# Vision layer on one core: the attention memory term made per group inside the loop instead of ahead of it

## The reference, cut to what matters

```python
sq = jax.nn.elu(q) + 1.0
A_mem = jnp.einsum('bhsd,hde->bhse', sq, mem) / (jnp.einsum('bhsd,hdo->bhso', sq, z) + 1e-06)
g = jax.nn.sigmoid(betas)
out = g * A_mem + (1.0 - g) * attn
out = out.transpose(0, 2, 1, 3).reshape(b, s, d)
out = out @ Wo.T + bo
```

## Time and profile before

| what | value |
|---|---|
| median of 3 runs | 249.62 us (249.26 to 251.57) |
| the profiled execution | 249.06 us, its span 247.3 us |
| mean granted clock of PE over the span | 0.912 of full |
| PE busy | 210.5 us, 85% |
| DVE, ACT, POOL busy | 88.7, 76.2, 54.9 us |

### The profile page before, as it was taken

How to read it: one execution, slowest core, us unless ns; L and a number is a source line. 1 busy time by engine, 2 the same in 40 slices (tenths; PEclk the granted TensorE clock), 3 DMA queues, 4 the chain that set the end, 5 groups by cost and what they waited for, 6 DMA issues and landing times.

```text
span 247.3 us, 3565 instructions
## 1 busy us (share of the span) xinstructions
PE 210.5 (85%) x1307; PEld 187.7 (76%) x1307; DVE 88.7 (36%) x279; ACT 76.2 (31%) x224; POOL 54.9 (22%) x55
## 2 busy tenths in 40 slices
PE   0185956989998785989999999999999999999970
PEld 0185956965766454459999999999999999999970
DVE  6849874443678654203211111111111111111120
ACT  2433311634554114023622232322222323222220
POOL 0245343000004446300004004022040040220404
PEclk9999995995579855599999999999999999999997
DMA  7935995520001322167429058095290580410211
GB/s 247 337 117 127 322 351 233 215 98 1 0 21 41 97 61 65 51 170 238 199 62 447 2 212 314 0 358 184 70 439 10 223 305 0 170 12 0 23 9 17
DMA packets 10299, 36.15 MB, mean 146 GB/s; under 512 B 3328, under 2 KB 6738, under 8 KB 7978
## 3 DMA queue, kind: packets, MB, share of 16 engines
q1 hardware_dynamic: 7514, 31.90, 35.7%
q0 software_dynamic: 2336, 2.13, 4.4%
q10 hardware_dynamic: 432, 1.90, 2.0%
HBM read 31.42 MB, written 5.35 MB: 149 GB/s over the span
## 4 chain that ended last, share of the span: by engine, by line
PE 74%; DVE 8%; DMA 5%; issue 4%; POOL 4%; ACT 2%; POOLq 1%; SPq 0%
PE bank L538 33%; PE bank L550 16%; DMA x_flat<-in 5%; PE bank L582 3%; PE bank L522 3%; DVE hn L793 3%; PE bank L469 2%; POOL token_rows L1027 2%; PE bank L424 2%; POOL rstd L1014 1%; PE bank L437 1%; PE bank L563 1%; PE bank L388 1%; PE bank L449 1%; PE bank L390 1%
## 5 line engine op out<-in xcount | busy, mean ns | idle before, releaser
L538 PE MATMUL bank<-xb,w 128*128 128x185 f32 x512 | 91.5, 322 | 1.1 <-ACT xb L710 1.1
L538 PEld LDWEIGHTS bank<-xb,w 128*128 128x128 f32 x512 | 81.9, 190 | 1.6 <-issue 1.2
L977 DVE TENSOR_TENSOR hid<-bank,sg 128x185 f32<-128x185 f32 x64 | 22.5, 351 | 113.4 <-ACT sg L722 113.4
L550 PE MATMUL bank<-hid,w 128*128 128x185 f32 x256 | 50.2, 319 | 0.0
L1044 POOL DMA_INDIRECT out<-yw,slot_token x16 | 23.8, 1489 | 118.3 <-ACT yw L742 109.1
L722 ACT ACTIVATE sg<-bank 128x185 f32<-128x185 f32 x64 | 20.9, 326 | 89.2 <-PE bank L538 89.2
L550 PEld LDWEIGHTS bank<-hid,w 128*128 128x128 f32 x256 | 42.1, 189 | 0.0
L337 PE MATMUL bank<-wp_hi,x_hi 128*111 128x256 f32 x36 | 11.2, 310 | 12.3 <-DVE x_lo L799 12.3
L337 PEld LDWEIGHTS bank<-wp_hi,x_hi 128*111 128x111 f32 x36 | 7.0, 194 | 12.5 <-issue 12.5
L1027 POOL DMA_INDIRECT token_rows<-rowbuf,dest x12 | 11.6, 968 | 13.4 <-DVE dest L936 11.6
L1035 POOL TENSOR_TENSOR rstd<-var,minus_half 111x1 f32<-111x1 f32 (+1 forms) x6 | 3.4, 571 | 34.3 <-DVE var L908 34.2
(11 more groups left out here) (145 smaller groups left out, 265.9 us busy)
## 6 DMA issues: line engine op xcount, KB each, us to landing
w<-in SPq DMA_DIRECT2D x8, 2048.0 KB, 10.6
w<-in SPq DMA_DIRECT2D x8, 1024.0 KB, 4.8
x_flat<-in SPq DMA_DIRECT2D x6, 333.0 KB, 10.7
token_rows<-rows_in SPq DMA_DIRECT2D x1, 1728.0 KB
rows_in<-token_rows SPq DMA_DIRECT2D x8, 144.0 KB
w_sb<-in ACTq DMA_DIRECT2D x1, 1024.0 KB, 8.6
wp_sb<-in ACTq DMA_DIRECT2D x1, 768.0 KB, 5.5
out<-h SPq DMA_DIRECT2D x5, 111.0 KB
```

Of the source, the lines that this page charges most:

```text
L538: mm = pe.matmul(o, w[:, part, k, :], xb[b][:, k, :], start=(k == 0), stop=(k == KD - 1))
L550: mm = pe.matmul(bank[YT_BANK[k]][:, 0:NS], w3[e % 2][:, fc, k * P:(k + 1) * P], hid[:, step % 4, :], start=(fc == 0), stop=(fc == FC - 1))
L977: dve.tensor_tensor(hid[:, step % 4, :], bank[GU_BANK[step % len(GU_BANK)]][:, NS:2 * NS], sg[:, step % 2, :], ALU.mult).then_inc(hid_done, 1)
```

## The change

The memory term leaves the place ahead of the loop; only the denominators stay there, now after the first two scores. The gate no longer weighs the denominators: DVE multiplies it into `mem_bd` before q comes. In the loop PE has a new stage `remember(g)` (lag 3, between `project` and `count`), which makes sq @ mem for one group with tokens on the partitions, in the upper half of the attention product's bank. DVE has a new stage `weigh_memory(g)` (lag 3, between `row_max` and `rank`), which multiplies it by the reciprocal denominators. `attend` begins with three more matmuls: one of zeros that opens the bank, and two with the identity that turn the weighed memory term into it; the attention product then accumulates on top. The sum needs no addition any more, so DVE's `add_memory` goes and ACT copies the bank to `aoT` (`copy_ao`, lag 4, first in its tuple). The constant `head_rows`, its DMA and its cast, the turn of the denominators and their copies go too. The diff, cut where it only declares or renumbers:

```diff
--- before.py
+++ after.py
         qneg = sb1("qneg", [P, 2, T])
         sqT = sb1("sqT", [P, 2, T])
-        memT = qneg
         den = sb1("den", [G_ROWS, GROUPS, HEADS])
-        den_split = sb1("den_split", [G_ROWS, GROUPS, 2, HEADS], F32R)
-        denT = sb1("denT", [2 * HEADS, T], F32R)
-        memgate = in_x_space(P, 1, 2, HALF)[:, 0]
+        mem_rows = in_x_space(G_ROWS, 2, HEADS, HD)
         probs = in_x_space(G_ROWS, 2, HEADS, G_ROWS)
         probsT = in_x_space(G_ROWS, 2, HEADS, G_ROWS)
         negmax = sb1("negmax", [G_ROWS, GROUPS, HEADS])
...
@@ -263,6 +257,7 @@
         S_BANK = ((0, 1), (2, 3))
         PT_BANK = 4
         PV_BANK, WO_BANK = 5, 6
+        MEM_AT = 512 - D
         ROUTER_BANK = 7
 
         block = ctx.enter_context(nc.Block())
...
@@ -402,27 +396,17 @@
                                        start=(m == 0), stop=(m == 1))
                 mm.then_inc(den_in_psum, 1)
 
-            def memory_turn():
-
-                pe.wait_ge(den_done, 1)
-                for g in range(GROUPS):
-                    R = ROWS[g]
-                    b, c = g // (GROUPS // 2), g % (GROUPS // 2) * G_ROWS
-                    tr = pe.transpose(bank[4 + b][0:2 * HEADS, c:c + R],
-                                      den_split[0:R, g, :, :].bitcast(F32).rearrange("p s h -> p (s h)"), ident[0:R, 0:R])
-                tr.then_inc(denT_in_psum, 1)
-
-            def memory():
-
-                pe.wait_ge(denT_done, 2)
-                for n, (m, hf) in enumerate(WIDE):
-                    if n == 0:
-                        pe.wait_ge(k_done, 4)
-                    if n >= 2:
-                        pe.wait_ge(mem_done, n - 1)
-                    pe.matmul(bank[4 + n % 2][:, 0:HALF], head_rows_r[:, m, :], denT[:, half(hf)], start=True, stop=True)
-                    pe.matmul(bank[6 + n % 2][:, 0:HALF], mem_bd[:, m, :], sqT[:, m, half(hf)],
-                              start=True, stop=True).then_inc(mem_in_psum, 1)
+            def remember(g):
+
+                R = ROWS[g]
+                if g == 0:
+                    pe.wait_ge(mem_gated, 1)
+                else:
+                    pe.wait_ge(ao_done, g)
+                for m in range(2):
+                    mm = pe.matmul(bank[PV_BANK][0:R, MEM_AT + m * P:MEM_AT + (m + 1) * P], sqT[:, m, cols(g)], mem_bd[:, m, :],
+                                   start=True, stop=True)
+                mm.then_inc(mem_in_psum, 1)
 
             def score(g):
                 R = ROWS[g]
...
@@ -442,7 +426,7 @@
                 R = ROWS[g]
                 pe.wait_ge(pn_done, g + 1)
                 if g == 0:
-                    pe.wait_ge(mem_done, 4)
+                    pe.wait_ge(den_done, 2)
                 if g >= 1:
                     pe.wait_ge(pT_done, g)
                 for hd in range(HEADS):
@@ -451,13 +435,16 @@
 
             def attend(g):
                 R = ROWS[g]
+                pe.wait_ge(mem_done, g + 1)
+                pe.matmul(bank[PV_BANK][:, 0:2 * R], zero_bf[:, 0:P], zero_bf[:, 0:2 * R], start=True, stop=False, skip_group_check=True)
+                for m in range(2):
+                    pe.matmul(bank[PV_BANK][:, m * R:(m + 1) * R], mem_rows[0:R, g % 2, 2 * m:2 * m + 2, :].rearrange("p h c -> p (h c)"),
+                              ident[0:R, 0:R], start=False, stop=False, skip_group_check=True)
                 pe.wait_ge(pT_done, g + 1)
-                if g >= 1:
-                    pe.wait_ge(ao_done, g)
                 for hd in range(HEADS):
                     rows = slice(HD * (hd % 2), HD * (hd % 2) + HD)
                     mm = pe.matmul(bank[PV_BANK][rows, (hd // 2) * R:(hd // 2 + 1) * R],
-                                   v_sb[0:R, g, hd * HD:(hd + 1) * HD], probsT[0:R, g % 2, hd, 0:R], start=True, stop=True)
+                                   v_sb[0:R, g, hd * HD:(hd + 1) * HD], probsT[0:R, g % 2, hd, 0:R], start=False, stop=True, skip_group_check=True)
                 mm.then_inc(pv_done, 1)
 
             def project(g):
...
@@ -497,15 +484,13 @@
                 pe.wait_ge(hot_done, g + 1)
                 pe.matmul(o, before_bf[0:R, 0:R], hot[0:R, g, :], start=False, stop=True).then_inc(count_done, 1)
 
-            memory_den()
             pe.wait_ge(k_done, 4)
             pe.wait_ge(mask_set, 1)
             score(0)
             score(1)
-            memory_turn()
-            memory()
+            memory_den()
             for t in range(GROUPS + 7):
-                for lag, stage in ((6, route), (3, turn_probs), (4, project), (6, count), (5, turn_xn), (0, score), (3, attend)):
+                for lag, stage in ((6, route), (3, turn_probs), (4, project), (3, remember), (6, count), (5, turn_xn), (0, score), (3, attend)):
                     if 0 <= t - lag < GROUPS and not (stage == score and t - lag < 2):
                         stage(t - lag)
 
...
@@ -687,19 +672,17 @@
                                        scale=gamma_t[:, k:k + 1], bias=beta_t[:, k:k + 1])
                 a.then_inc(xnT_done, 1)
 
-            act.wait_ge(denT_in_psum, 1)
-            first = GROUPS // 2 * G_ROWS
-            act.activation(denT[:, 0:first], bank[4][0:2 * HEADS, 0:first], ACT.Copy).then_inc(denT_done, 1)
-            act.activation(denT[:, first:T], bank[5][0:2 * HEADS, 0:T - first], ACT.Copy).then_inc(denT_done, 1)
+            def copy_ao(g):
+                R = ROWS[g]
+                act.wait_ge(pv_done, g + 1)
+                if g >= 2:
+                    act.wait_ge(wo_done, g - 1)
+                act.activation(aoT[:, g % 2, :, 0:R], bank[PV_BANK][:, 0:2 * R].rearrange("p (m c) -> p m c", m=2),
+                               ACT.Copy).then_inc(ao_done, 1)
+
             softmax(0)
-            for n in range(len(WIDE)):
-
-                act.wait_ge(mem_in_psum, n + 1)
-                if n >= 2:
-                    act.wait_ge(mem_done, n - 1)
-                act.activation(memgate[:, n % 2, :], bank[4 + n % 2][:, 0:HALF], ACT.Copy).then_inc(memgate_done, 1)
             for t in range(GROUPS + 7):
-                for lag, stage in ((1, softmax), (5, copy_xnT), (2, copy_probsT)):
+                for lag, stage in ((4, copy_ao), (1, softmax), (5, copy_xnT), (2, copy_probsT)):
                     if 0 <= t - lag < GROUPS and not (stage == softmax and t - lag < 1):
                         stage(t - lag)
             GU_BANK, YT_BANK, XB_BANK, Y_BANK = (0, 1, 2, 7), (3, 4), 5, 6
...
@@ -840,7 +823,9 @@
             dve.wait_ge(gate_exp, 1)
             then(dve.tensor_scalar(gate[:, :], gate[:, :], 1.0, None, ALU.add))
             then(dve.reciprocal(gate[:, :], gate[:, :]))
-            then(dve.tensor_scalar(keep[:, :], gate[:, :], -1.0, 1.0, ALU.mult, ALU.add))
+            dve.tensor_scalar(keep[:, :], gate[0:G_ROWS, :], -1.0, 1.0, ALU.mult, ALU.add)
+            mem_heads = mem_bd[:, :, :].rearrange("p m (h c) -> p (m h) c", h=2)
+            dve.tensor_tensor(mem_heads, mem_heads, gate[:, :].unsqueeze(2).broadcast_to([P, HEADS, HD]), ALU.mult).then_inc(mem_gated, 1)
 
 
             for n, (m, hf) in enumerate(WIDE):
@@ -865,17 +850,19 @@
                 dve.wait_ge(den_in_psum, 1)
                 full = (GROUPS - 1) * HEADS
                 den2 = den[:, :, :].rearrange("p g h -> p (g h)")
-                dve.tensor_scalar(den2[:, 0:full], bank[4][0:G_ROWS, 0:full], 1e-6, None, ALU.add)
-                then(dve.tensor_scalar(den2[0:ROWS[-1], full:full + HEADS], bank[4][0:ROWS[-1], full:full + HEADS], 1e-6, None, ALU.add))
+                dve.tensor_scalar(den2[:, 0:full], bank[4][0:G_ROWS, 0:full], 1e-6, None, ALU.add).then_inc(den_done, 1)
+                dve.tensor_scalar(den2[0:ROWS[-1], full:full + HEADS], bank[4][0:ROWS[-1], full:full + HEADS], 1e-6, None,
+                                  ALU.add).then_inc(den_done, 1)
+                dve.wait_ge(den_done, 2)
                 then(dve.reciprocal(den2, den2))
-                then(dve.tensor_tensor(den[:, :, :], den[:, :, :], gate[:, :].unsqueeze(1).broadcast_to([G_ROWS, GROUPS, HEADS]), ALU.mult))
-                then(dve.tensor_copy(den_split[:, :, 0, :], den[:, :, :]))
-                dve.tensor_tensor(den_split[:, :, 1, :], den[:, :, :], den_split[:, :, 0, :].bitcast(F32),
-                                  ALU.subtract).then_inc(den_done, 1)
-
-            def memory_part(n, m, hf):
-                dve.wait_ge(memgate_done, n + 1)
-                dve.tensor_tensor(memT[:, m, half(hf)], bank[6 + n % 2][:, 0:HALF], memgate[:, n % 2, :], ALU.mult).then_inc(mem_done, 1)
+
+            def weigh_memory(g):
+                R = ROWS[g]
+                dve.wait_ge(mem_in_psum, g + 1)
+                if g >= 2:
+                    dve.wait_ge(pv_done, g - 1)
+                dve.tensor_tensor(mem_rows[0:R, g % 2, :, :], bank[PV_BANK][0:R, MEM_AT:MEM_AT + D].rearrange("p (h c) -> p h c", h=HEADS),
```

(17 more changed lines are left out.)

27 lines of the change are left out of this document (10 added, 17 removed).

## The result

The changed kernel takes 267.35 us (median of 4 runs, 266.2 to 273.24) against 249.44 us (249.1 to 251.57, 4 runs) of the kernel before on the same chip: a ratio of 1.068, 95% interval 1.060 to 1.077. It is 17.9 us slower; 9.2 us slower was forecast, and the range ended at 264.5.

A forecast was written before the change was run, and what follows sets the result against it. It took a ring through the engines to set the loop's pace, with PE full in the experts' stage. Head -6.9 and loop +16.6 give +9.7: 249.06 + 9.7 = 258.8 us, range 250.5 to 264.5.

The forecast's parts named there:

- both waits: In each loop step, waits of about 1 us on ACT (copy_ao) and about 2 on DVE (weigh_memory).
- with the clock granted at the times of before: Loop sum assumed the old profile's clock changes: 2.4 GHz, 1.2 (57 to 70.6), 2.4 (to 84.3), 1.2 (to 105).
- the new products: PE's memory product, zeros and turning products add about 1.0 us per loop step at 2.4 GHz, 1.9 at 1.2.
- the head: Ahead of the loop: first turn of probabilities at 55.5 instead of 62.43, a gain of 6.9 us.
- rival without an earlier head: First turn of probabilities not earlier, denominators still waited for; only the loss is left, 266 us; chance 0.05.
- The copy on ACT: copy_ao behind copy_probsT delays the projection to 1.5 us after the turn; PE idle 0.8 to 1.1 us, steps 4 to 8.
- The wait on DVE: Weighing waits for remember, so ranking comes after projection, memory product and weighing; about 2 us in each step.
- the ring: Steps 6 to 8, between turns of normalised rows: 6.9 us at 2.4 GHz against 4.71, 10.3 at 1.2 against 5.46.
- The POOL ring: Rival: POOL's ring, about 4.4 us per step, remains the loop's bound and hides the new work; 242.2 us; chance 0.07.
- the middle: Chosen price of the zeros and two turning products per step: 0.55 us at 2.4 GHz, 1.05 at 1.2.
- low all through: Rival: clock falls early and stays at 1.2 GHz, each ring 10.3 us, loop ends at 116; 266 us; chance 0.09.
- The signs to look for: Profile checks: first turn, L456's idle time, L864's wait, spacing of turns, loop's end at 105 to 113 us.

The follow-up runs named there:

- e3: Changed kernel with ACT's copy to aoT moved ahead of the copy that waits and DVE's weighing moved behind the ranking; 249.38 us, ratio 0.996 to the kernel before.
- e2: Changed kernel with only DVE's weighing moved behind rank, norm2 and send of the same step; 261.37 us, ratio 1.043 to the kernel before.
- e6: e3 plus products that nobody reads in PE's list, around the count and in steps 9 to 12; 251.84 us, ratio 1.003 to the kernel before.
- e5: Changed kernel plus products that nobody reads, put into PE's waits from step 4 on; 263.45 us, ratio 1.052 to the kernel before.
- e7: Changed kernel with the memory term left out of the output and ACT's copy to aoT moved early; 242.88 us, ratio 0.972 to the kernel before.
- e8: Kernel before the change plus the same unread products as e6; 252.73 us, ratio 1.006 to the kernel before.

## Why the prediction was wrong, by its own steps

The direction, the places and the causes were right: both waits stand where the prediction put them, and e3 shows that they are the loss. The step that failed is the clock, "with the clock granted at the times of before"; a term of the sum, the new products, was also too small. The time was 8.6 us too low: 1.2 in the head, 5.5 in the loop, 1.3 outside the span, and 0.5 by which the profiled execution lies under the median.

*The head.* Forecast -6.9, measured -5.7. The k product ended 0.95 us later in this execution (its last piece at 50.09 + 0.15, against 49.29), and the scores start at 50.74. In the other profiles with this head this last piece lies anywhere from 48.73 (e2) to 50.39 (e6), and no run says why. From there to the turn it is 5.96 us; 5.7 was forecast (49.78 to 55.5), though its own terms add up to 55.3. What the forecast left out is that PE's third score (54.90 to 56.54) stands ahead of the turn as well and ends nearly as late as DVE: PE waited for only 0.16 us. The denominators took 2.37 instead of 2.09. The rival without an earlier head falls.

*The copy on ACT.* Forecast 1.5 us from turn to projection with 0.8 to 1.1 us idle; measured 1.50 and 0.88. Right.

*The wait on DVE and the ring.* Forecast 6.9 us at 2.4 GHz and 10.3 at 1.2. Measured 10.51 and 10.15 at 1.2; the one ring at 2.4 GHz, 7.85, also holds the last group's score (0.44), which leaves 7.4. The POOL ring hid nothing, as forecast. (The parts that the prediction lists as PE's add up to 3.85 us, which doubled would give 10.7 rather than 10.3; it took "some 3.4".)

*The new products.* This term was mis-sized. `remember` was forecast at 0.45 and 0.88 us and measured 0.45 and 0.86. The zeros with the two turning products were forecast at 0.55 and 1.05 us; the chain of waits has:

```profile
57.79 0.85 PE bank L407 x4
...
60.03 0.29 PE bank L439
60.32 1.13 PE bank L441 x4
```

and in the timeline at 2.4 GHz they fill 0.20 + 0.63 us. That is 0.83 and 1.42, the upper bound of the range (0.8 and 1.4), not the middle which I took; over six groups some 2 us (an estimate: three groups at 1.2 GHz, two at 2.4, and the short last one). The prediction had cited the Trainium skill ("TensorE: Matmul & The Clock Gate", Part 2, step by step) for the rule that the next weights load while a matmul runs, by which columns alone would count. The trace doesn't agree for L441: at the same clock it takes 1.13 us for 444 columns in four matmuls, where L407 takes 0.85 for 512. The loaded weights differ (128 columns against 111), but so do the rows that are summed over (111 against 128) and that L441 adds to what is in the bank; no run separates them, so the cause stays open.

*The clock.* This is the step that failed: "with the clock granted at the times of before". Against the forecast, the loop from first turn to end lost 5.5 us more. By turns of probabilities, step by step (forecast, measured): 3.7, 5.6; 7.9, 7.5; 7.2, 6.5; 6.9, 8.7; 8.5, 10.9; and from the last turn to the end 19.2, 19.8. The three large misses are where the clock was already low (it fell at 54.5 instead of 57) or fell earlier and stayed low (from 82 to 119.5, instead of 84.3 to 105). Two of the 5.5 us are the sizes above; the other 3.5 are what is left, and I put them down to the clock. The first step bears this out. In the kernel before it ran wholly at 1.2 GHz:

```profile
65.77 1.09 PE L449 MATMUL bank<-ident,x_flat 111*111 111x111 f32 x4
```

From 62.43 to there it is 3.34 us; with the prediction's own prices at 1.2 GHz (0.88 + 1.05) it comes to 5.3, and 3.7 was forecast, because half of the step was put at 2.4. For the second stretch, e3 shows that it hangs on the waits: without them the clock stood low for 17 us there instead of 37.5. The waits that I had priced empty PE, and I then priced the clock as if PE were as full as before. The early first fall is not their doing: in e3 the clock falls at 54.5 as well. The rival "low all through" had the right sign, and with its 266 us it was close, but by luck, since it isn't what happened: between 68.5 and 82 us the clock was high.

*Outside the span* lie 3.0 us instead of 1.8. I had no term for that, and no run explains it: the runs of the changed kernel have 2.4 to 3.1.

*The signs to look for* otherwise came as written: first turn near 55.5 (56.7), L456 idle five times (4.1 us in all), L864 waiting for L407, rings of 7.9 to 10.5 for groups 1 to 3, the experts' stage unchanged. Missed were the ring after these (6.24, with 4.4 to 5.5 forecast) and the loop's end (115.6, with 105 to 113).

## What to carry to other kernels

When a chain of one engine's instructions is spread over steps, ask of each instruction in a static order what it stands behind, not only what it waits for: a copy of 0.35 us whose data were long there, and a weighing of 0.42 us, cost 18 us by their places alone, and moving two tuple entries gave all of it back. Taken out together, two such waits gave back 18.0 us, and one by one 14.6 in all (a difference at the edge of the noise), so undo suspected waits together too. And a forecast that adds waits to PE has to move the clock with them; the granted clock of the old profile belongs to the old idle times.

## What the runs showed of the hardware that I had not expected

Adding unread products to PE made the changed kernel 3.9 us faster (e5), where the clock stood at 2.4 GHz all through a stretch of 34 us. Leaving the memory term's products out (54 of the 264 matmuls of the changed kernel between 54.5 and 119.5 us) did not raise it: from 54 to 103 us it stood at 1.2 GHz for 31 us in e7 and for 27 in e3, which has these products. The same filling did nothing for a loop with few waits (e6, e8), and it let a filler that is paced in matmuls end too early: the busy passes took 4.45 us instead of 6.48, the clock fell during the wait for the DMA that followed, and this cost 2.5 us in the experts' stage.

No long wait went ahead of the clock's fall: in the changed kernel it fell at 82 us and stayed low to the loop's end, and no single wait of PE in the loop is longer than 0.88 us.

Four matmuls of 111 columns with 128-column weights took more than four of 128 columns with 111-column weights, 1.13 against 0.85 us at 1.2 GHz and 0.63 against 0.45 at 2.4.
